# Moving the third row of max scores between the value products of two key blocks

## The reference, cut to what matters

```python
q = qkv[..., :2 * Hx].reshape(Bx, 2 * NQ, Sx, HD)      # 32 heads of 8
k = jnp.repeat(k, 2 * NQ // NKV, axis=1)                # from 8 heads
v = jnp.repeat(v, NQ // NKV, axis=1)
scores = jnp.einsum('bhqd,bhkd->bhqk', q, k) / math.sqrt(HD)
scores = jnp.where(causal, scores, -jnp.inf)
aw = jax.nn.softmax(scores, axis=-1)
aw = aw[:, :, 0] - lam * aw[:, :, 1]
attn = jnp.einsum('bhqk,bhkd->bhqd', aw, v) * (1.0 - LAMBDA_INIT)
```

## Time and profile before

| what | value |
|---|---|
| median of 3 runs | 624.63 us (623.15 to 624.79) |
| span of the profiled execution | 636.2 us |
| mean granted TensorE clock in it | 0.884 |
| the second attention's loop in it | about 199 to 439 us |
| PE busy, share of the span | 511.2 us, 80% |
| DVE busy | 422.6 us, 66% |
| ACT busy | 333.1 us, 52% |
| POOL busy | 310.1 us, 49% |

### The profile page before, as it was taken

How to read it: one execution, slowest core, us unless ns; L and a number is a source line. 1 busy time by engine, 2 the same in 40 slices (tenths; PEclk the granted TensorE clock), 3 DMA queues, 4 the chain that set the end, 5 groups by cost and what they waited for, 6 DMA issues and landing times. The chain is left out here.

```text
span 636.2 us, 12685 instructions
## 1 busy us (share of the span) xinstructions
PE 511.2 (80%) x3814; PEld 346.9 (55%) x3814; DVE 422.6 (66%) x1653; ACT 333.1 (52%) x559; POOL 310.1 (49%) x472
## 2 busy tenths in 40 slices
PE   4978569924488999999999999998471899998970
PEld 2657469922233444454454544444361888888870
DVE  4875737625577799999999999936348344434446
ACT  5654236605424477777777777775331443434333
POOL 2541054247431386655685567554200565656540
PEclk9998579976677699999999999999655899999995
DMA  9400022222744246657435444230650111111205
GB/s 330 165 2 34 33 47 72 61 71 63 154 66 95 43 96 134 146 105 174 122 86 141 106 104 91 73 79 20 247 134 35 45 38 47 41 45 43 42 30 198
DMA packets 90411, 58.18 MB, mean 91 GB/s; under 512 B 72661, under 2 KB 76758, under 8 KB 88458
## 3 DMA queue, kind: packets, MB, share of 16 engines
q1 hardware_dynamic: 81994, 41.31, 25.8%
q0 software_dynamic: 3744, 7.68, 4.8%
q10 hardware_dynamic: 4608, 8.39, 3.7%
HBM read 37.72 MB, written 19.63 MB: 90 GB/s over the span
## 5 line engine op out<-in xcount | busy, mean ns | idle before, releaser
L1663 DVE CUSTOM_DVE_ANT_1 banks<-banks,a_mask 128x480 f32<-128x480 f32 (+14 forms) x480 | 189.7, 457 | 14.8 <-PE banks L1890 12.9
L1790 ACT ACTIVATE a_prob_<-banks 128x1024 f32<-128x1024 f32 x160 | 154.8, 1022 | 48.5 <-PE banks L1904 48.5
L1526 POOL TENSOR_SCALAR_AFFINE_SELECT a_prob_<-a_prob_ 128x512 f32<-128x512 f32 x128 | 80.8, 635 | 83.3 <-ACT a_prob_ L1790 82.4
L1890 PE MATMUL banks<-a_k_u_,a_q_u_ 72*128 72x512 bf16 (+15 forms) x512 | 107.1, 303 | 4.9 <-DVE a_neg_max_ L1663 3.9
L1191 PE MATMUL banks<-f_hgt,f_w_now 128*112 128x128 f32 (+1 forms) x808 | 102.9, 280 | 8.9 <-ACT f_w_now L1118 8.9
L1890 PEld LDWEIGHTS banks<-a_k_u_,a_q_u_ 72*128 72x128 bf16 x512 | 65.0, 148 | 72.9 <-DVE a_neg_max_ L1663 39.9
L1191 PEld LDWEIGHTS banks<-f_hgt,f_w_now 128*112 128x112 f32 (+1 forms) x808 | 96.0, 185 | 12.3 <-issue 12.2
L1904 PE MATMUL banks<-a_q_u_,a_k_x_ 75*128 75x512 bf16 x320 | 100.1, 394 | 2.2 <-DVE a_coef_p L1646 1.6
L952 POOL DMA_INDIRECT f_hg<-scratch_h_rows,r_source x62 | 59.7, 963 | 78.9 <-DVE r_source L292 48.9
L1916 PE MATMUL banks<-a_prob_,a_v_g_ 128*32 128x512 f32 (+3 forms) x1024 | 84.7, 448 | 0.4 <-POOL a_prob_ L1526 0.4
L1663 DVE DVE_READ_ACCUMULATOR2_ANT a_neg_max_<- 128x1 f32 x512 | 71.4, 141 | 0.0
(11 more groups left out here) (233 smaller groups left out, 646.8 us busy)
## 6 DMA issues: line engine op xcount, KB each, us to landing
a_q_u_<-scratch_q_parts SPq DMA_DIRECT2D x16, 576.0 KB
scratch_o_rows<-a_o_sb_ ACTq DMA_DIRECT2D x28, 256.0 KB, 2.6
w<-in_w SPq DMA_DIRECT2D x2, 2048.0 KB, 10.1
w<-in_w SPq DMA_DIRECT2D x2, 1792.0 KB, 10.1
scratch_q_parts<-a_part_ SPq DMA_DIRECT2D x24, 128.0 KB
a_k_u_<-scratch_k_parts SPq DMA_DIRECT2D x48, 48.0 KB
scratch_h_rows<-r_h SPq DMA_DIRECT2D x8, 256.0 KB, 2.0
f_back<-scratch_back_rows SPq DMA_DIRECT2D x4, 512.0 KB, 5.2
```

The costliest lines, as they stand in the source:

```text
L1526: nc.gpsimd.affine_select(out=block_p, in_=block_p, pattern=[[0, JH], [1, P]], compare_op=ALU.is_ge, fill=0.0, base=0, channel_multiplier= ...
L1663: last = nc.vector.tensor_tensor_reduce(out=found, in0=found, in1=mask[:, :, TG - 4 * (t + 1):], scale=-1.0, scalar=-MASKED, op0=ALU.add, ...
L1790: nc.scalar.activation(prob[g % 2][:, 2 * e:2 * e + 2].rearrange("p s j t c -> p (s j) t c"), PS[:, b0:b0 + 2, :].rearrange("p s (j c t) - ...
L1890: last = nc.tensor.matmul(PS[:, a % 3, off:off + width], queries[:, g % 2, :, t], k_u[r][:, :, g % 2 * TG:g % 2 * TG + 4 * (t + 1)], start ...
```

## The change

In turns 1 to 28, row 2 of the max scores is issued behind the value products of key block 1 and ahead of those of blocks 2 and 3; before, it stood behind all three. No instruction is added, removed or resized, and no wait is changed in the program. In turn 0 there are no value products, and from turn 29 on there are no rows, so the order there is the same.

```diff
@@ -1994,9 +1994,11 @@
                 scores(g, 1)
                 rows(1)
                 if g >= 1:
-                    for kb in range(1, NQ):
+                    values(g - 1, 1)
+                rows(2)
+                if g >= 1:
+                    for kb in range(2, NQ):
                         values(g - 1, kb)
-                rows(2)
                 scores(g, 2)
                 rows(3, 4)
                 if g > GROUPS - 3:
```

## The result

| kernel | median | runs |
|---|---|---|
| before | 624.71 us | 623.15 to 624.91, 4 runs |
| after | 633.17 us | 630.89 to 634.70, 4 runs |

The ratio is 1.0137, with a 95% interval of 1.0111 to 1.0162: the change costs 8.5 us. The profiled execution of after took 634.7 us with a span of 633.0 us. In one experiment, e10, three of the ten runs (636.19, 638.41 and 643.24 us) were slower at a lower granted clock, and its ratio leaves them out.

What follows compares the result with a forecast made beforehand. TensorE's cycle with the last exponential was taken to bound the steady turn; 24 turns x 0.28 us for an extra visit made 6.7 us, so 624.63 + 6.7 = 631.3 us, range 626.0 to 634.5 us.

Steps and rivals of the forecast that it cites:

- TensorE's cycle sets the turn, not VectorE: Second attention's steady turn: last exponential 1.08, TensorE from scores 1 to scores 4 5.33, then 0.65, together 7.06 us.
- The rule on emptying PSUM: Rival in the steady turn: VectorE, emptying PSUM, is the bound; 8.3 us faster, 616.3 us; chance 0.08.
- VectorE's wait moves to row 3: VectorE's 0.36 us wait ahead of row 2 goes and returns ahead of row 3, some 0.6 us (0.36 + 0.28).
- The price of a visit: One extra TensorE visit to the column strips in values 1 to 3: 0.28 us a turn, bounds 0.20 and 0.37.
- going in behind row 2: TensorE's switch from undivided rows into strips: 0.08 us lost behind row 1, 0.09 behind row 5.
- 0.12 inside: Within each visit to the values, 0.12 us remain beyond 1.72 ns a column, however many blocks it has.
- coming out: TensorE's switch from strips to undivided rows: about 0.055 us lost at row 2, 0.05 at row 6.
- the estimate that the prediction worked out from the drain: Two drains of some 0.053 us in 24 turns: 2.6 us, 627.2 us in all; the rows show more than twice that.
- Which turns pay: 23 steady turns and turn 1 pay 0.28 us each, 6.7 us; turns 2, 11, 19 and 27 pay nothing.
- the clock as a rival: In the loop, a half-clock spell of 12 us comes back: 6 us on top, 637.3 us; chance 0.02.
- The span: First to last instruction in a profile like that of before, 636.2 us: 642.9 us after the change.
- ScalarE's copy: Result copy behind value block 3 ends near 312.4, tying with scores 2 at 312.39; exponential 2 follows at no cost.

Runs made afterwards that it cites:

- e10: The change plus VectorE reducing only the first half of each granule's columns, against the kernel before: 624.76 us over all ten runs, ratio 0.9979.
- e4: Order of the kernel before, with VectorE taking maxima over only the first half of each granule's columns: 618.87 us, ratio 0.991 to before.
- e2: Kernel before with row 2 between value blocks 1 and 2 and row 3 between blocks 2 and 3, so three visits before scores 2: 641.27 us, ratio 1.0276.
- e11: Half reductions as in e4, with values 0 held for the next turn's visit, one visit a turn fewer: 609.49 us, ratio 0.9764 to before.
- e5: Kernel before with row 6 and scores 4 issued ahead of values 0, no visit added or saved: 624.87 us, ratio 0.9996.
- e6: The change together with e5's move of values 0 behind scores 4, against the kernel before: 634.72 us, ratio 1.0138.
- e7: Kernel before with row 2 moved ahead of all three value blocks, directly behind row 1, still two visits a turn: 634.46 us, ratio 1.0159.

## Why the prediction was right, point by point

- **TensorE's cycle sets the turn, not VectorE.** Shown: with VectorE's work down from 6.63 to 4.78 us a turn the turn stayed at 7.06 us (e4), and a visit more or fewer moved it (e2, e10, e11). The rule on emptying PSUM that the prediction named ("TensorEngine Tiling (Array Packing)", section PSUM Bottleneck, in the Trainium skill) doesn't bind here in the steady turns; in turns 11, 19 and 27 VectorE does set the time, as e4 shows. Nor is VectorE far behind: in e5 row 6, moved ahead of values 0, waits for it.
- **VectorE's wait moves to row 3 and grows by the price of the visit.** 0.36 + 0.28 = 0.64 was forecast, 0.64 us stands in the trace, and over the loop 14.5 us in 23 waits, 0.63 each.
- **The price of a visit.** 0.28 us was taken from the edges of the old visits; it measures 0.26 for the first extra one, 0.29 for the second, 0.25 in another order (e6 against e5). Of the sub-terms two hold, 0.10 going in behind row 2 (forecast 0.08) and 0.12 inside; coming out is 0.02 where 0.05 was read from the old edges. The terms of the prediction make 0.25 (0.08 + 0.12 + 0.05), so the 0.28 that it took was more than they gave. Its 0.12 us inside a visit came from two visits and two unknowns, so that these agreed proved nothing; the new visits are the test. By 1.72 ns a column and 0.12 us, 384 columns make 0.78 us and 256 make 0.56; measured are 0.78 twice in after and 0.57 in e2.
- **What the price is made of.** That TensorE loses time at every change between strips and the undivided array agrees with the Trainium skill ("TensorEngine Tiling (Array Packing)", section Key Properties); 0.26 us for a pair of changes is over twice the estimate that the prediction worked out from the drain on the Trainium skill's page "TensorE: Matmul & The Clock Gate" (section "Step-by-step: what each phase is for"). Every change here is one of operand type as well, bf16 to 32-bit and back; no run parts the two, so which of them costs the time is open.
- **Which turns pay.** 23 steady ones, turn 1 by about 0.1 us (9.37 and 9.32 us, where the three profiles of before have 9.34, 9.23 and 9.10), turn 2 nothing (7.53 us in both), turns 11, 19 and 27 nothing (8.1 us). 23 x 0.26 = 6.0 us, the measured difference of the loops; forecast were 6.7 in 24 turns.
- **The total.** 631.3 us was forecast, 633.17 us came. The loop's term was 0.7 us too large, and a term was missing: 2.7 us behind the loop, almost a third of the measured change, where the clock came out differently. The prediction had the clock as a rival inside the loop only and put the stages behind it at nothing without a reason. That the total came within 1.9 us is in part luck, since the two errors point opposite ways.
- **The span.** 642.9 us was forecast for the profile, 633.0 came. The sum was made on a profile of before that was some 12.6 us long in the experts' stage; working it as a difference and adding it to the median kept that out of the forecast time.
- **ScalarE's copy** tied with scores 2 as forecast. Exponential 2 starts 0.52 us behind the start of the copy without a gap of its own, and costs nothing:

```profile
315.28 0.59 ACT L1801 COPY a_o_sb_<-banks 128x512 f32<-128x512 f32 x1 [1.03 <-PE banks L1916]
315.80 1.02 ACT L1790 ACTIVATE a_prob_<-banks 128x1024 f32<-128x1024 f32 x1
```

What stays open is why the clock behind the loop, and the time there, comes out one way for before and another for after; that 2.7 us of the change is measured, and its cause isn't shown.

## What to carry to other kernels

An engine that is 94% busy and has one visible wait a turn is not thereby the bound: follow the wait that closes the cycle from one turn to the next, and look at a turn in which the suspected engine has more to do. Before moving an instruction between others, count how often the engine changes its mode; here each extra pair of changes between 32-bit column strips and the undivided bf16 array cost 0.25 to 0.29 us, more than VectorE's whole wait was worth to the turn. Ask as well what the moved instruction itself waits for: in e7 row 2, and in e5 row 6, came too early for VectorE, and TensorE paid for it. Working out a difference inside the stage, and not from the span, keeps a profile's own oddities elsewhere out of the sum.

## What the hardware showed that was not expected

- The granted clock behind the loop: 0.79 in the first 8 us there for after, 1.00 for before, and the full clock back later at the experts' start; 2.7 us in all. Neither a later end of the loop (e7) nor the order of the rows (e4) decides which of the two comes.
- The clock can fall inside the loop. In the profile of e5 turn 27, in which TensorE waited for VectorE, was followed by the half clock, and turns 27 and 28 took 10.4 and 9.6 us. After turns 11 and 19 there and turns 11, 19 and 27 of e6, which took 8.33 to 8.35 us, no half clock followed. The stretches about turn 27 of e5:

```profile
400.00:404.00 4.00, 3.30 (x32) 1.23 (x29) 3.96 (x16) 3.41 (x4) 2.47 (x6) 1.00 0.30 64
404.00:408.00 4.00, 3.92 (x18) 1.32 (x18) 3.42 (x17) 2.05 (x2) 1.58 (x3) 0.68 0.27 56
408.00:412.00 4.00, 4.00 (x20) 1.61 (x20) 2.49 (x15) 1.46 (x2) 0.96 (x3) 0.50 0.02 6
```

- Short undivided products in a run go at the pace of long ones when nothing holds them up: four of 160 to 352 columns, 1024 in all, took 0.43 us in e11, where 1024 columns in two products take 0.45.
